# An attention and feed-forward layer in fp32: start of the first batch reordered (wq ahead of x, scaling folded into the halves of wq, bv times wo ahead of V, K's first copies issued by ScalarE)

## The chip, the cores and the metric

The kernel runs on one core of one Trainium2 chip. A core has five engines that run side by side: TensorE (PE in the profile, with PEld for its weight loads), VectorE (DVE), ScalarE (ACT), GpSimd (POOL) and SyncE (SP), which here only issues transfers. 16 DMA engines move data. The metric is device time in microseconds (us), lower is better. The kernel before takes 2871.87 us, the median of 3 runs (2871.01 to 2873.98).

## The reference

For each of 16 sequences of 512 rows and width 512:

```
q = layer_norm(x, ln1_g, ln1_b)
qh = (q @ wq + bq), kh = (ctx @ wk + bk), vh = (ctx @ wv + bv)   # 16 heads of 32
scores = qh @ kh^T / sqrt(32), causal mask, softmax
x1 = x + (probs @ vh) @ wo + bo
h = layer_norm(x1, ln2_g, ln2_b)
out = x1 + gelu(h @ w1 + b1) @ w2 + b2                            # inner width 2048
```

Everything is fp32.

## The kernel before

**Two stages.** stage_a does attention for all 16 batches and ends near 1480 us; stage_b does the feed-forward part. Only the start of stage_a is changed, the part that is done once, before and in the first batch.

**Precision.** Dense products are split: each fp32 operand is held as a high half in fp32r (made by a cast, _hi) and the remainder (_lo). A product is three matmuls: hi·hi, lo·hi, hi·lo. ScalarE makes the high halves (weight_high, x_high, qk_high), VectorE the low ones (weight_low, x_low, qk_low), GpSimd both for the context (context, lines 791 to 798).

**Folding of the layer norm's vectors.** ln1_g and the factor -1/sqrt(32) go into wq: before, VectorE writes wq_scaled (four instructions of 128x512 at line 615, in the space of v_sb), from which ScalarE casts wq_hi and VectorE makes wq_lo. ln1_b goes into a bias: TensorE multiplies the raw wq by ln1_b with 32 matmuls of one column (line 495, bias_mm), VectorE adds bq and scales (lines 630, 632). bv and bo are folded into one row: job B multiplies bv, spread over 128 columns (bvx), by the raw wo (line 383), and VectorE adds it to bo_row (line 673). The raw weights lie in buffers that are used for other things later: wq and wo share pT, wk has the rest of pT, wv has sm.

**Prologue.** The list PRO gives TensorE's order: X0 to X3 (transposes of the normalised rows, line 378), Q0, K0 (12 matmuls of 512 columns each, line 427), V0a (24 of 256 columns, line 422). Each job writes one of three banks bank_d in turn, and waits until the bank's last reader is done. ScalarE and VectorE have their own hand-written order of the same work. The queue of SP issues vec, x (four tiles), wq, two context tiles, wk, wv, bo, two more context tiles (each when its buffer is free), wo, then the copies for Q0 and K0.

**Stacks.** The scores take the three products at once: 96 rows stack hi, lo and hi of 32 features. So each Q0 or K0 (st_hi, st_lo) is copied into stack by three transfers of 256 KB (stack_parts, line 270): two from st_hi, once qk_high is done, and one from st_lo, once qk_low is done. The first score waits for all six.

**Batches.** A batch has 4 groups of 12 steps. At each step TensorE does the score of a tile, then its share of a dense job from BESIDE (in group 0 of the first batch: B, Q1, K1, V1a), then the transpose of the probabilities three tiles back. VectorE masks and takes the minimum (line 590), ScalarE takes the exponential (line 727). The copies for the next group's Q and K are issued as soon as they are made, and the next group's first score waits for them.

Of the kernel before, what the change touches and what calls it, by code (L numbers as in the profile page):

```python
# [20 lines left out]
F32 = mybir.dt.float32  # L21
# [31 lines left out]
def stage_a(nc, x, ctxT, wq, wk, wv, wo, vecs, bo, x1):  # L53
# [16 lines left out]


    COUNT = {"X": 4, "Q": 12, "K": 12, "V": 24, "R": 4, "O": 12, "B": 4}
    PRO = ["X0", "X1", "X2", "X3", "Q0", "K0", "V0a"]


    BESIDE = [
# [13 lines left out]
    def beside(groups, first, last):  # L90

        steps = [[] for _ in range(TG * len(groups))]
        for g, jobs in enumerate(groups):
            for job, at in jobs:
                if job == "R" and first and g == 0 or job == "B" and not first or job[0] == "O" and first:
                    continue
                if last and (job[0] == "X" or job in ("Q0", "K0", "V0a")):
                    continue
                done = 0
                for k, n in at.items():  # L100
                    steps[TG * g + k].append((job, done, done + n))
                    done += n
                assert done == COUNT[job[0]]
        return steps
# [3 lines left out]
    with ExitStack() as ctx:  # L108
# [11 lines left out]
        w_lo = [sb(f"{n}_lo", [P, KT, D], F32R) for n in ("wq", "wk", "wv", "wo")]  # L120
        vec = sb("vec", [P, 5, 4])
        bqs = sb("bqs", [P, NG])
        bo_row = sb("bo_row", [P, D])
        xt = sb("xt", [P, QT, D])
        xnT_hi = sb("xnT_hi", [P, KT, S], F32R)
# [25 lines left out]
        raw = [pT_flat[:, 0:KT * D], pT_flat[:, KT * D:2 * KT * D], sm[:].rearrange("p t n -> p (t n)"),  # L151
               pT_flat[:, 0:KT * D]]
        assert SLOTS_S * 512 == KT * D
        wq_scaled = v_sb[:].rearrange("p t n -> p (t n)")
        bvx = rT[:].rearrange("p (t m) -> p t m", t=KT)

        bank_s = [pb(f"bank_s{i}") for i in range(BANKS_S)]
# [100 lines left out]
        def _(sp):  # L258
# [23 lines left out]
            def load_x(m, t):  # L282
                sp.dma_start(xt[:, t, :], one(x_v, m)[:, t, :]).then_inc(x_in[t], 16)

            for t in range(QT):
                load_x(0, t)

            def load_weight(i):
                sp.dma_start(raw[i].rearrange("p (t n) -> p t n", t=KT),
                             (wq, wk, wv, wo)[i].rearrange("(t p) n -> p t n", p=P)).then_inc(raw_in[i], 16)  # L290

            load_weight(0)
            load_c(0, 0)
            load_c(0, 1)
            load_weight(1)
# [3 lines left out]
            load_c(0, 2)  # L299
            sp.wait_ge(c_done, 2)  # L300
            load_c(0, 3)
            sp.wait_ge(scaled, KT)
            sp.wait_ge(bias_mm, 1)
            load_weight(3)
            for w, job in enumerate(("Q0", "K0")):
                stack_parts(pro, w, job, 0, 0, 0)

            def stacks(it, g):

# [52 lines left out]
        def _(pe):  # L362
# [121 lines left out]

            pe.sem_inc(transposed, SLOTS_S)
            pe.sem_inc(pv_done, 2)
            pe.wait_ge(consts, 1)
            for job in PRO:
                if job == "Q0":

                    pe.wait_ge(vec_in, 16)
                    pe.wait_ge(raw_in[0], 16)
                    for g in range(NG):
                        for kt in range(KT):
                            mm = pe.matmul(bank_s[0][:, g:g + 1], raw[0][:, D * kt + P * g:D * kt + P * g + P],
                                           vec[:, 1, kt:kt + 1], start=(kt == 0), stop=(kt == KT - 1))
                    mm.then_inc(bias_mm, 1)
                    pe.wait_ge(w_lo_done, 1)
                if job == "K0":
                    pe.wait_ge(w_lo_done, 2)  # L500
                if job == "V0a":
                    pe.wait_ge(w_lo_done, 3)
                dense_step(pro, job, 0, 0, COUNT[job[0]])

            def body(it):
# [35 lines left out]
        def _(dve):  # L541
# [65 lines left out]
                dve.sem_inc(d_free[i], 1)  # L607
            dve.wait_ge(vec_in, 16)
            V.tensor_copy(bvx, vec[:, 4, :].unsqueeze(2).to_broadcast([P, KT, P])).then_inc(bvx_ok, 1)
            for t in range(QT):  # L610
                layer_norm_stats(0, t)
            dve.wait_ge(raw_in[0], 16)
            for kt in range(KT):

                V.tensor_scalar(wq_scaled[:, D * kt:D * kt + D], raw[0][:, D * kt:D * kt + D],
                                vec[:, 0, kt:kt + 1], -SCALE, ALU.mult, ALU.mult).then_inc(scaled, 1)
            for t in range(QT):
                normalise(0, t)

            def weight_low(i, done):  # L620
                dve.wait_ge(w_hi_done, i + 1)
                V.tensor_tensor(w_lo[i][:].rearrange("p t n -> p (t n)"), raw[i] if i else wq_scaled,
                                w_hi[i][:].rearrange("p t n -> p (t n)").bitcast(F32),
                                ALU.subtract).then_inc(done, 1)

            weight_low(0, w_lo_done)
            for t in range(QT):
                x_low(pro, f"X{t}", 0, 0)
            dve.wait_ge(bias_mm, 1)
# [1 line left out]
            dve.wait_ge(bias_ok, 1)  # L631
            V.tensor_scalar(bqs[:], bqs[:], -SCALE, None, ALU.mult).then_inc(scaled, 1)
            weight_low(1, w_lo_done)
            dve.wait_ge(scaled, KT + 1)
            qk_low(pro, "Q0", 0, 0)
            weight_low(2, w_lo_done)
            qk_low(pro, "K0", 0, 0)
            weight_low(3, wo_lo_done)
            dve.wait_ge(consts, 2)

            def body(it):
                for n in range(len(it.steps) + it.tail):
                    g, k = divmod(n, TG)
                    if (n > LAG and not it.tail or n <= LAG and not it.first) and not act_moves(n - LAG - 1):
                        move_tile(dve, V.tensor_copy, it, n - LAG - 1)
                    if not it.tail:
                        mask_and_max(it, n)
                    for job, jg in it.ended(n):
                        if job[0] == "X":
                            x_low(it, job, jg, it.b + 1)  # L650
                    beside_previous = g < NG and not (it.first and g == 0) and n < len(it.steps)
                    if k == 1 and beside_previous:

                        dve.wait_ge(probs, it.b * TB + TG * g)
                        V.reciprocal(recips[:, (g - 1) % 2, :], sums[:, (g - 1) % 2, :]).then_inc(recip_ok, 1)
                    if k == O_PROD_AT and beside_previous:
                        o_product(it, g - 1)
                    if not it.last and not it.tail:
                        for t in range(QT):
                            if (g, k) == STATS_AT[t]:  # L660
                                layer_norm_stats(it.b + 1, t)
                        for t in range(QT):
                            if (g, k) == NORMALISE_AT[t]:
                                normalise(it.b + 1, t)
                    for job, jg in it.ended(n - 1):

                        if job[0] in "QK":
                            qk_low(it, job, jg, it.b * NG + (jg + 1))
                    for job, jg in it.ended(n):
                        if job == "B":  # L670
                            dve.wait_ge(dense, it.done(job, jg))
                            dve.wait_ge(bo_in, 16)
                            V.tensor_tensor(bo_row[:], bank_d[it.bank(job, jg)][:], bo_row[:],
                                            ALU.add).then_inc(d_free[it.bank(job, jg)], 1)
                        if job[0] == "O":
                            t, bank = int(job[1]), it.bank(job, jg)
                            dve.wait_ge(dense, it.done(job, jg))

                            dve.wait_ge(res_ok, it.b * QT + (t + 1 - QT))
                            V.tensor_tensor(xt[:, t, :], bank_d[bank][:], xt[:, t, :],  # L680
                                            ALU.add).then_inc(d_free[bank], 1)
# [5 lines left out]
        def _(act):  # L687
# [54 lines left out]

            def weight_high(i):
                act.wait_ge(raw_in[i], 16)
                A.copy(w_hi[i][:].rearrange("p t n -> p (t n)"), raw[i] if i else wq_scaled).then_inc(w_hi_done, 1)

            act.wait_ge(scaled, KT)
            weight_high(0)
            for t in range(QT):
                x_high(pro, f"X{t}", 0)  # L750
            weight_high(1)
            act.wait_ge(scaled, KT + 1)
            qk_high(pro, "Q0", 0, 0)
            weight_high(2)
            qk_high(pro, "K0", 0, 0)
            weight_high(3)
            v_copy(pro, "V0a", 0)

# [29 lines left out]
        def _(pool):  # L788
# [23 lines left out]
            def o_low(it, g):  # L812
# [12 lines left out]

            G_.affine_select(out=mask[:, 384:512], in_=mask[:, 384:512], compare_op=ALU.is_ge, fill=MASKED, base=0,
                             pattern=[[-1, P]], channel_multiplier=1).then_inc(consts, 1)
            for fb in range(2):
                context(0, fb)
            inverse_root(0)  # L830
            for fb in (2, 3):
                context(0, fb)

            def body(it):
# [18 lines left out]
                expand(it, 2)  # L853
                o_low(it, 2)
                if it.first:
                    pool.wait_ge(d_free[it.bank("B", 0)], it.bank_read("B", 0))
                pool.wait_ge(res_in, it.b * 16 + 16)
                for t in range(QT):
                    G_.tensor_tensor(out=xt[:, t, :], in0=xt[:, t, :], in1=bo_row[:],
# [870 lines left out]
```

## Time and profile before

| | |
|---|---|
| median of 3 runs | 2871.87 us |
| the profiled execution | 2871.73 us |
| its span, first to last instruction | 2870.0 us |
| outside the span | 1.73 us |
| TensorE busy | 2766.4 us (96%) |
| VectorE, ScalarE, GpSimd busy | 70%, 58%, 12% |
| first matmul | 17.38 us |
| first score | 50.05 us |
| mean granted TensorE clock | 0.988 of 2.4 GHz |

A busy TensorE at 96% means that nearly all of the span is matmuls, one behind another; what can be taken out is found where TensorE is idle or works without need. That is read from the timeline (each instruction's start and duration), the list of who waited for whom, and the busy time of each engine in stretches. Matmul durations in the timeline overlap: of a row of equal matmuls, the distance from start to start is what one costs.

### The profile page before, as it was taken

To read this page: it belongs to the slowest core of one execution; us is meant where nothing else is said; L and a number is where in the kernel's file an instruction comes from. 1 tells how busy PE (TensorE), PEld (TensorE's weight loads), DVE (VectorE), ACT (ScalarE), POOL (GpSimd) and SP (SyncE) were. 2 spreads that over 40 slices of the span, in tenths; PEclk is the share of its full clock that TensorE was granted. 3 is DMA by queue.
4 is the path that set the end of the run, shared out by engine and by line. 5 is a ranking of instruction groups with operands and counts; after the bars stand their busy time and mean duration, and the time that the engine had idled before them with its cause. 6 is when DMAs were issued, how large, how long until landed. Compare 5 with 4: busy or idle time off the path is not lost. (4 is left out here: it accounts for less than half of the span.)

```text
span 2870.0 us, 65737 instructions
## 1 busy us (share of the span) xinstructions
PE 2766.4 (96%) x22056; PEld 2513.9 (88%) x22056; DVE 2016.5 (70%) x4852; ACT 1678.4 (58%) x4046; POOL 356.1 (12%) x364
## 2 busy tenths in 40 slices
PE   6999999999999999999957999999999999999999
PEld 4788888888888888888847999999999999999999
DVE  4777777776777777777648778778778755666566
ACT  3666666666766666666635655655665544444444
POOL 1211222112222222222110000000000000000000
PEclk9999999999999999999988999999999999999999
DMA  6667767776676667766632543443455334433342
GB/s 141 113 124 113 117 115 126 121 111 121 114 126 121 105 123 117 124 124 111 97 119 96 191 171 129 175 188 131 156 190 206 132 116 154 159 135 142 126 161 96
DMA packets 152506, 383.03 MB, mean 133 GB/s; under 512 B 12928, under 2 KB 17024, under 8 KB 144256
## 3 DMA queue, kind: packets, MB, share of 16 engines
q1 hardware_dynamic: 152448, 382.28, 54.5%
q8 instruction: 34, 0.56, 0.1%
q14 instruction: 24, 0.20, 0.0%
HBM read 172.51 MB, written 109.05 MB: 98 GB/s over the span
## 5 line engine op out<-in xcount | busy, mean ns | idle before, releaser
L727 ACT ACTIVATE sm<-sm,mins 128x128 f32<-128x128 f32 (+3 forms) x1024 | 572.2, 559 | 463.2 <-DVE mins L590 458.0
L590 DVE CUSTOM_DVE_ANT_0 sm<-bank_s,mask 128x128 f32<-128x128 f32 (+3 forms) x1024 | 475.5, 484 | 120.6 <-PE bank_s L442 118.8
L537 DVE COPY pT<-bank_t 128x384 f32<-128x384 f32 (+1 forms) x544 | 307.7, 566 | 240.1 <-PE bank_t L454 240.0
L454 PE MATMUL bank_t<-ident,sm 128*128 128x128 f32 x2560 | 412.7, 275 | 6.9 <-ACT pT L537 3.4
L454 PEld LDWEIGHTS bank_t<-ident,sm 128*128 128x128 f32 x2560 | 306.6, 140 | 87.9 <-issue 30.6
L442 PE MATMUL bank_s<-stack 96*128 96x128 f32 (+3 forms) x1024 | 352.8, 385 | 13.7 <-DMA stack<-st_lo 11.6
L1115 PE MATMUL bank_x<-b_hi,w_hi 128*128 128x256 f32 x1024 | 294.8, 288 | 18.0 <-ACT g L1538 9.6
L1115 PE MATMUL bank_x<-w_hi,a_hi 128*128 128x256 f32 x1024 | 291.2, 284 | 3.5 <-DVE a_lo L1235 3.5
L1117 PE MATMUL bank_x<-b_hi,w_lo 128*128 128x256 f32 x1024 | 291.7, 285 | 0.0
L1116 PE MATMUL bank_x<-b_lo,w_hi 128*128 128x256 f32 x1024 | 291.6, 285 | 0.0
L1116 PE MATMUL bank_x<-w_lo,a_hi 128*128 128x256 f32 x1024 | 290.8, 284 | 0.0
L1117 PE MATMUL bank_x<-w_hi,a_lo 128*128 128x256 f32 x1024 | 290.7, 284 | 0.0
L1549 ACT ACTIVATE g<-g,vecb 128x256 f32<-128x256 f32 x384 | 174.7, 503 | 111.3 <-DVE g L1316 109.3
L1563 ACT CAST a_hi<-g 128x512 fp32r<-128x512 f32 x256 | 158.7, 621 | 116.1 <-PE bank_x L1117 93.7
L1115 PEld LDWEIGHTS bank_x<-b_hi,w_hi 128*128 128x128 f32 x1024 | 198.1, 193 | 20.1 <-DVE w_lo L1235 11.4
L1115 PEld LDWEIGHTS bank_x<-w_hi,a_hi 128*128 128x128 f32 x1024 | 197.8, 193 | 4.0 <-DVE xr L1360 3.6
L1116 PEld LDWEIGHTS bank_x<-b_lo,w_hi 128*128 128x128 f32 x1024 | 198.5, 194 | 0.0
L1117 PEld LDWEIGHTS bank_x<-b_hi,w_lo 128*128 128x128 f32 x1024 | 198.4, 194 | 0.0
L1116 PEld LDWEIGHTS bank_x<-w_lo,a_hi 128*128 128x128 f32 x1024 | 197.8, 193 | 0.0
L1117 PEld LDWEIGHTS bank_x<-w_hi,a_lo 128*128 128x128 f32 x1024 | 197.7, 193 | 0.0
L727 ACT ACTIVATION_READ_ACCUMULATOR sm<-sm,mins 128x1 f32 x1024 | 192.1, 188 | 0.0
L442 PEld LDWEIGHTS bank_s<-stack 96*128 96x128 f32 x1024 | 175.0, 191 | 18.7 <-DMA stack<-st_lo 11.6
(178 smaller groups left out, 7423.8 us busy)
## 6 DMA issues: line engine op xcount, KB each, us to landing
stack<-st_hi SPq DMA_DIRECT2D x256, 256.0 KB, 6.1
stack<-st_lo SPq DMA_DIRECT2D x128, 256.0 KB, 8.1
xr<-x_scratch SPq DMA_DIRECT2D x32, 1024.0 KB, 5.9
b_scratch<-b_hi SPq DMA_DIRECT2D x16, 1792.0 KB, 9.9
b_scratch<-b_lo SPq DMA_DIRECT2D x16, 1792.0 KB, 13.7
b_hi<-b_scratch SPq DMA_DIRECT2D x16, 1792.0 KB, 7.4
b_lo<-b_scratch SPq DMA_DIRECT2D x16, 1792.0 KB, 11.2
xt<-in_x SPq DMA_DIRECT2D x64, 256.0 KB, 2.7
```

The source lines that it names most:

```text
L442: mm = pe.matmul(bank_s[n % BANKS_S][:, off:off + w], stack[0:96, g % 2, 0, r, P * qt:P * qt + P], stack[0:96, g % 2, 1, r, 0:w], start=Tr ...
L454: mm = pe.transpose(bank_t[n % 2][:, P * c:P * c + P], sm[:, n % SLOTS_S, P * c:P * c + P], ident[:])
L537: copy(out, src).then_inc(moved[n % 2], 1)
L590: op = V.tensor_tensor_reduce(sm[:, n % SLOTS_S, off:off + w], bank_s[n % BANKS_S][:, off:off + w], mask[:, 512 - w:512], 1.0, 0.0, ALU.ad ...
L727: op = A.activation(row, row, ACT.Exp, bias=mins[:, g % 2, c:c + 1], scale=-1.0, accum_out=sums[:, g % 2, c:c + 1])
L1115: pe.matmul(o, lh, rh, start=opens, stop=False, skip_group_check=True)
L1116: pe.matmul(o, lh, rl, start=False, stop=False, skip_group_check=True)
L1117: return pe.matmul(o, ll, rh, start=False, stop=True, skip_group_check=True)
L1549: op = A.activation(to, bank_x[d][:, C * m:C * m + C] if name == "C21" else to, ACT.Gelu, bias=vec[:, f:f + 1], scale=1.0)
L1563: A.copy(a_part(a_hi, k, h), a_source(k, h)).then_inc(a_hi_ok, 1)
```

## The change

Five edits, all in what is done once:

- SP issues wq ahead of the four tiles of x. TensorE's 32 matmuls for the bias (line 495) stand ahead of everything, in front of its wait for the constants.
- wq_scaled is gone. VectorE writes a vector wq_scale of 4 columns, ScalarE makes wq_hi in four activations of 128x512 with that scale, VectorE makes wq_lo in four scalar_tensor_tensor of 128x512, ahead of the layer norm's statistics.
- Job B moves from group 0 of the first batch into the prologue, between K0 and V0a; its addition to bo_row moves along.
- K0's copies are issued by ScalarE (stack_keys), not by SP. wv_hi is made ahead of Q0's high half.
- GpSimd takes the inverse root ahead of the context tiles; the load of wo waits for the halves of wq.

```
-    PRO = ["X0", "X1", "X2", "X3", "Q0", "K0", "V0a"]
+    PRO = ["X0", "X1", "X2", "X3", "Q0", "K0", "B", "V0a"]
...
             load_weight(0)
+            for t in range(QT):
+                load_x(0, t)
             load_c(0, 0)
...
-            sp.wait_ge(scaled, KT)
+            sp.wait_ge(w_lo_done, KT)
             sp.wait_ge(bias_mm, 1)
             load_weight(3)
-            for w, job in enumerate(("Q0", "K0")):
-                stack_parts(pro, w, job, 0, 0, 0)
+            stack_parts(pro, 0, "Q0", 0, 0, 0)
...
+            V.tensor_scalar(wq_scale[:], vec[:, 0, :], -SCALE, None, ALU.mult).then_inc(scaled, 1)
+            for kt in range(KT):
+                dve.wait_ge(w_hi_done, kt + 1)
+                V.scalar_tensor_tensor(w_lo[0][:, kt, :], raw[0][:, D * kt:D * kt + D], wq_scale[:, kt:kt + 1],
+                                       w_hi[0][:, kt, :].bitcast(F32), ALU.mult, ALU.subtract).then_inc(w_lo_done, 1)
             for t in range(QT):
                 layer_norm_stats(0, t)
...
+            def stack_keys():
+
+                def copy(part, src):
+                    act.dma_start(stack[32 * part:32 * part + 32, 0, 1, :, :].bitcast(F32),
+                                  src[:, 1, :].bitcast(F32)).then_inc(stacked, 16)
+
+                act.wait_ge(qk_hi, 2)
+                copy(0, st_hi)
+                copy(2, st_hi)
+                act.wait_ge(d_free[pro.bank("K0", 0)], pro.bank_read("K0", 0))
+                copy(1, st_lo)
+
+            act.wait_ge(scaled, 1)
+            act.wait_ge(raw_in[0], 16)
+            for kt in range(KT):
+                A.activation(w_hi[0][:, kt, :], raw[0][:, D * kt:D * kt + D], ACT.Identity, bias=0.0,
+                             scale=wq_scale[:, kt:kt + 1]).then_inc(w_hi_done, 1)
             for t in range(QT):
                 x_high(pro, f"X{t}", 0)
             weight_high(1)
-            act.wait_ge(scaled, KT + 1)
+            weight_high(2)
+            act.wait_ge(scaled, 2)
             qk_high(pro, "Q0", 0, 0)
-            weight_high(2)
             qk_high(pro, "K0", 0, 0)
+            stack_keys()
             weight_high(3)
             v_copy(pro, "V0a", 0)
...
-            for fb in range(2):
-                context(0, fb)
             inverse_root(0)
-            for fb in (2, 3):
+            for fb in range(KT):
                 context(0, fb)
```

## Rows read from the trace of the kernel before

**Rows 1.** Windows: stretch, length, busy us of PE, PEld, DVE, ACT, POOL, clock, DMA share, GB/s.
```profile
0.00:20.00 20.00, 2.62 (x12) 2.42 (x12) 10.03 (x19) 4.35 (x4) 7.74 (x15) 1.00 0.80 276
...
160.00:180.00 20.00, 20.00 (x139) 15.91 (x141) 13.72 (x43) 11.41 (x33) 0.61 (x1) 1.00 0.72 121
```

**Rows 2.** Waits of TensorE, 0 to 120 us: total, times, longest.
```profile
PE bank_d L378 <- DVE xt L560: 17.4, 1, 17.4
PE bank_s L442 <- DMA stack<-st_lo: 10.8, 3, 7.5
```

**Rows 3.** Timeline (start, duration, what, idle before) up to the inverse root.
```profile
7.70 0.69 DVE L547 BATCH_NORM_STATS2 stats<-xt 128x6 f32<-128x512 f32 x1 [0.84 <-DMA xt<-in_x]
...
8.76 0.17 DVE L555 TENSOR_SCALAR ve<-mv 128x4 f32<-128x4 f32 x1
10.78 3.06 DVE L615 TENSOR_SCALAR v_sb<-pT,vec 128x512 f32<-128x512 f32 x4 [1.85 <-DMA pT<-in_wq]
10.83 1.28 ACT L745 ACT_TABLE_LOAD   x1 [10.83 <-DMA pT<-in_wq]
...
15.62 1.02 POOL L803 TENSOR_TENSOR rstd<-ve,nhalf 128x4 f32<-128x4 f32 x1
```

**Rows 4.** The same timeline, the transposes of x and the bias.
```profile
17.38 2.79 PE L378 MATMUL bank_d<-ident,xt 128*128 128x128 f32 x12 [17.38 <-DVE xt L560]
18.50 0.59 ACT L693 CAST xnT_hi<-bank_d 128x512 fp32r<-128x512 f32 x1 [2.73 <-PE bank_d L378]
18.51 2.29 DVE L622 TENSOR_TENSOR wq_lo<-v_sb,wq_hi 128x2048 fp32r<-128x2048 f32 x1
18.63 2.64 POOL L795 CAST cT_hi<-c_raw 128x512 fp32r<-128x512 f32 x1 [1.99 <-DMA c_raw<-in_ctxT]
...
20.71 1.88 DVE L568 TENSOR_TENSOR xnT_lo<-bank_d,xnT_hi 128x512 fp32r<-128x512 f32 x3
...
22.36 6.83 PE L495 MATMUL bank_s<-vec,pT 128*128 128x1 f32 x32
...
23.23 0.69 DVE L568 TENSOR_TENSOR xnT_lo<-bank_d,xnT_hi 128x512 fp32r<-128x512 f32 x1 [0.63 <-ACT xnT_hi L693]
23.25 1.27 POOL L797 TENSOR_TENSOR cT_lo<-c_raw,cT_hi 128x512 fp32r<-128x512 f32 x1
```

**Rows 5.** The same timeline, Q0's first matmul to job B.
```profile
29.05 0.77 PE L427 MATMUL bank_d<-xnT_hi,wq_hi 128*128 128x512 f32 x1
...
34.62 0.69 ACT L703 ACTIVATE st_hi<-bank_d,bqs 128x512 fp32r<-128x512 f32 x1 [9.62 <-PE bank_d L427]
...
35.33 1.33 SPq L270 DMA_DIRECT2D stack<-st_hi  x2
...
40.11 0.55 SPq L270 DMA_DIRECT2D stack<-st_lo  x1
...
40.70 1.09 SPq L264 DMA_DIRECT2D c_raw<-in_ctxT  x2
...
50.05 0.80 PE L442 MATMUL bank_s<-stack 96*128 96x128 f32 x2 [7.46 <-DMA stack<-st_lo]
...
50.64 5.92 PE L383 MATMUL bank_d<-pT,rT 128*128 128x512 f32 x8
```

**Rows 6.** Windows: the wait for the first stack, and a later stretch at half clock.
```profile
37.50:48.00 10.50, 3.11 (x25) 2.91 (x24) 4.84 (x3) 3.06 (x3) 0.00 (x0) 0.86 1.07 132
...
76.00:79.00 3.00, 3.00 (x12) 2.51 (x11) 0.81 (x5) 1.61 (x6) 0.00 (x0) 0.50 0.01 3
```

**Rows 7.** Timeline: two matmuls of Q1, its copies, the second group's first score.
```profile
56.63 0.39 PE L427 MATMUL bank_d<-xnT_lo,wq_hi 128*128 128x512 f32 x1
56.86 0.40 PE L427 MATMUL bank_d<-xnT_hi,wq_lo 128*128 128x512 f32 x1
...
60.67 1.26 SPq L270 DMA_DIRECT2D stack<-st_hi  x2
...
74.36 0.50 PE L442 MATMUL bank_s<-stack 96*128 96x128 f32 x2 [2.39 <-DMA stack<-st_lo]
```

More of the change, by code:

```diff
@@ L94, in beside @@
             for job, at in jobs:
-                if job == "R" and first and g == 0 or job == "B" and not first or job[0] == "O" and first:
+                if job == "R" and first and g == 0 or job[0] == "O" and first:
                     continue
@@ L122, in stage_a @@
         bqs = sb("bqs", [P, NG])
+        wq_scale = sb("wq_scale", [P, KT])
         bo_row = sb("bo_row", [P, D])
@@ L153, in stage_a @@
         assert SLOTS_S * 512 == KT * D
-        wq_scaled = v_sb[:].rearrange("p t n -> p (t n)")
         bvx = rT[:].rearrange("p (t m) -> p t m", t=KT)
@@ L283, in load_x @@
                 sp.dma_start(xt[:, t, :], one(x_v, m)[:, t, :]).then_inc(x_in[t], 16)
-            for t in range(QT):
-                load_x(0, t)
             def load_weight(i):
@@ L486, in _ @@
             pe.sem_inc(pv_done, 2)
+            pe.wait_ge(vec_in, 16)
+            pe.wait_ge(raw_in[0], 16)
+            for g in range(NG):
+                for kt in range(KT):
+                    mm = pe.matmul(bank_s[0][:, g:g + 1], raw[0][:, D * kt + P * g:D * kt + P * g + P],
+                                   vec[:, 1, kt:kt + 1], start=(kt == 0), stop=(kt == KT - 1))
+            mm.then_inc(bias_mm, 1)
             pe.wait_ge(consts, 1)
@@ L489, in _ @@
                 if job == "Q0":
[L491 to L498, printed above, removed]
+                    pe.wait_ge(w_lo_done, KT)
                 if job == "K0":
-                    pe.wait_ge(w_lo_done, 2)
+                    pe.wait_ge(w_lo_done, KT + 1)
                 if job == "V0a":
-                    pe.wait_ge(w_lo_done, 3)
+                    pe.wait_ge(w_lo_done, KT + 2)
                 dense_step(pro, job, 0, 0, COUNT[job[0]])
@@ L609, in _ @@
             V.tensor_copy(bvx, vec[:, 4, :].unsqueeze(2).to_broadcast([P, KT, P])).then_inc(bvx_ok, 1)
+            V.tensor_scalar(wq_scale[:], vec[:, 0, :], -SCALE, None, ALU.mult).then_inc(scaled, 1)
[3 more added lines that the diff above has]
+                                       w_hi[0][:, kt, :].bitcast(F32), ALU.mult, ALU.subtract).then_inc(w_lo_done, 1)
             for t in range(QT):
                 layer_norm_stats(0, t)
[L612 to L616, printed above, removed]
             for t in range(QT):
@@ L620, in weight_low @@
             def weight_low(i, done):
-                dve.wait_ge(w_hi_done, i + 1)
-                V.tensor_tensor(w_lo[i][:].rearrange("p t n -> p (t n)"), raw[i] if i else wq_scaled,
+                dve.wait_ge(w_hi_done, KT + i)
+                V.tensor_tensor(w_lo[i][:].rearrange("p t n -> p (t n)"), raw[i],
                                 w_hi[i][:].rearrange("p t n -> p (t n)").bitcast(F32),
                                 ALU.subtract).then_inc(done, 1)
-            weight_low(0, w_lo_done)
             for t in range(QT):
@@ L633, in _ @@
             weight_low(1, w_lo_done)
-            dve.wait_ge(scaled, KT + 1)
+            dve.wait_ge(scaled, 2)
             qk_low(pro, "Q0", 0, 0)
@@ L637, in _ @@
             qk_low(pro, "K0", 0, 0)
+            dve.wait_ge(dense, pro.done("B", 0))
+            dve.wait_ge(bo_in, 16)
+            V.tensor_tensor(bo_row[:], bank_d[pro.bank("B", 0)][:], bo_row[:],
+                            ALU.add).then_inc(d_free[pro.bank("B", 0)], 1)
             weight_low(3, wo_lo_done)
@@ L669, in body @@
                     for job, jg in it.ended(n):
[L670 to L674, printed above, removed]
                         if job[0] == "O":
@@ L744, in weight_high @@
                 act.wait_ge(raw_in[i], 16)
-                A.copy(w_hi[i][:].rearrange("p t n -> p (t n)"), raw[i] if i else wq_scaled).then_inc(w_hi_done, 1)
-            act.wait_ge(scaled, KT)
-            weight_high(0)
+                A.copy(w_hi[i][:].rearrange("p t n -> p (t n)"), raw[i]).then_inc(w_hi_done, 1)
+            def stack_keys():
[9 more added lines that the diff above has]
+            act.wait_ge(raw_in[0], 16)
+            for kt in range(KT):
+                A.activation(w_hi[0][:, kt, :], raw[0][:, D * kt:D * kt + D], ACT.Identity, bias=0.0,
+                             scale=wq_scale[:, kt:kt + 1]).then_inc(w_hi_done, 1)
             for t in range(QT):
@@ L855, in body @@
                 if it.first:
-                    pool.wait_ge(d_free[it.bank("B", 0)], it.bank_read("B", 0))
+                    pool.wait_ge(d_free[pro.bank("B", 0)], pro.bank_read("B", 0))
                 pool.wait_ge(res_in, it.b * 16 + 16)
```

2 rows, old and new, of the table BESIDE are left out of this document.

## The prediction

> **What bounds the kernel now.** I read the windows first. From 160 us on TensorE is busy through all of a 20 us stretch, in the first 20 us it has 2.62 us of work [rows 1]: the steady part is bound by TensorE, the start by what comes before it. So a microsecond taken from the start should be kept to the end, and nothing else in this change touches the steady part. Then the list of TensorE's waits: 17.4 us for the first normalised rows, and 10.8 us for the low parts of stacks, 7.5 of it once, before the first score [rows 2]. Then the timeline, to follow what each of these two waits for.
>
> The first wait: x has landed at 7.70, the variance is ready at 8.93, but the inverse root runs on GpSimd only from 15.62 to 16.64 [rows 3], behind two context tiles. The transposes start at 17.38. The low part of X0 starts only at 20.71, since VectorE makes wq_lo until then (18.51 to 20.80), and X3's transposes wait for it. x is finished at 23.92, but TensorE is in the 32 small bias matmuls from 22.36 [rows 4], and Q0 starts at 29.05 [rows 5].
>
> The second wait: Q0's copies are issued at 35.33, K0's last at 40.11, the first score starts at 50.05 [rows 5]. In between the DMA engines are full (share 1.07) and move 132 GB/s [rows 6]: six copies of 262 KB are 1.57 MB, 11.9 us at that rate, and with the time to the first byte and to the last signal they make 14.7 us from Q0's issue to the score. So the score hangs on when Q0's copies start, not on when K0's last one does. The second group repeats this: from Q1's copies at 60.67 to its first score at 74.36 are 13.7 us, with TensorE idle for the last 2.39 [rows 7].
>
> **Part 1: wq first, its halves and the inverse root.** In the kernel before x takes until 7.70 and wq 3.1 us more, until 10.78 [rows 3]. Turned round, wq lands between 5.5 (7.70 less part of the slow start) and 7.70, and x at about 10.8. I take 7.0 for wq. ScalarE's table load, 1.28 [rows 3], and four activations of about 0.6 to 0.7 (0.69 is the row of the same kind from PSUM [rows 5]) follow; VectorE ends the fourth low part 0.75 after the last: 7.0 + 1.3 + 2.7 + 0.8 = 11.8 (10.3 to 12.6). The statistics now stand behind that: four at 0.69, then 0.54 to the end of the variance [rows 3]: 15.1. GpSimd's root no longer stands behind context tiles: 16.2. Before it was 16.64. So a gain of 0.4; the bounds are x's landing (10.8 with three statistics done, a gain of 1.9) and a loss of 0.4. Transposes start at 17.0.
>
> VectorE has no wq_lo to do behind them, so X0's low part follows its high part, ready at 19.09, instead of 20.71: the stretch from first transpose to last low part, 6.54, shrinks by 1.6 to 4.9 [rows 4]. That ends at 21.9 and Q0 starts at 22.0, where before it started at 29.05: 7.0 earlier. The terms are 0.4 + 1.6 + 5.1 (the bias matmuls that stuck out behind x, 23.92 to 29.05). The bias matmuls now take 7.0 to 14, when TensorE has nothing else; if wq landed late, they would start to cost only beyond 10.
>
> GpSimd's context tiles are what pays for the root: they start at 16.2 instead of 11.5, and the next two loads are issued that much later. Before, the last ended at 24.52, with 2 us of waiting and a cast that took 2.64 us while VectorE ran wq_lo [rows 4]. So it ends between 24.5 and 29.4, I take 27. K0 needs it for its tenth matmul, about 29.8. No cost, but with only 3 us of cover.
> On that cast: 2.64 us beside a VectorE instruction of 2.29 [rows 4]. The Trainium skill (SBUF — State Buffer, "SBUF: two separate sides") says VectorE with two SBUF inputs and GpSimd lock each other out for a whole instruction. The trace agrees; by that rule wk_lo could stop one tile again, which is within the bound.
>
> **Part 2: Q0 to the first score.** Q0's twelve matmuls at half clock took 5.57 to its high part, 34.62 from 29.05, and 0.71 more to the copies [rows 5]. If it goes the same, the copies are issued at 22.0 + 6.3 = 28.3 to 28.4, against 35.33: 6.9 earlier. The clock could rise earlier in it; at the most it saves some 1.3 us. wv_hi, now ahead of Q0's high part, ends on ScalarE at about 25, under Q0.
>
> K0 ends at about 30.7, its high part is ready at 31.5, its low part at 32.3 behind wv_lo. By then the three copies of Q0 (6 us of DMA time from about 30.4) still run, so K0's copies come in time to keep the engines full, and again the sum of the transfers sets the end. ScalarE issuing them costs it about 0.6 us each, as SP's rows show [rows 5], under B and V0a: nothing.
> What is new: SP no longer waits for K0, so it issues the two context tiles for the next batch (at 40.70 before, behind all copies [rows 5]) right behind Q0's copies, ahead of K0's. They are 0.52 MB. If other lanes carry them they cost nothing; at the 276 GB/s of the first 20 us [rows 1] they cost 1.9. I take 0.6, nearer to none since loads move at more than twice the rate of the copies. First score: 28.4 + 14.7 + 0.6 = 43.7, a gain of 6.35. The 14.7 itself may be 13.7, as for the second group [rows 7].
> No row has a transfer issued by ScalarE. The Trainium skill (DMA: Bandwidth & Descriptors, "Issuing engines are not separate DMA queues") says that both run on the same 16 engines and only issue time is saved. By it this part brings nothing, which is also what my sum has; were it wrong, K0's 6 us would overlap Q0's (rival C).
>
> **Part 3: B.** It ran from 50.64 at half clock and held TensorE for 5.6 us between the first score and Q1. It now runs behind K0, at full clock (some 3.5 us), from 30.7 to 34.3; V0a follows to 37.1, both under the wait for the stack. wo is issued at about 21 and has landed. But its going doesn't give all of it, since the half clock that B sat in is now spent on Q1: from the first score to Q1's copies were 10.62 us (50.05 to 60.67 [rows 5, 7]). Now: 0.4 for the score, twelve matmuls at half clock (twice the 0.23 from start to start at full clock [rows 7], less a hair: 5.1), 0.4 for the second score, 0.9 to the copies: 6.8. A gain of 3.8. The second group hangs on these copies by 13.7 us, so this gain counts on. TensorE's own work in group 0 ends at about 62.5, before the stack at 64.3.
>
> **Sum.** 6.35 + 3.8 = 10.1 us. From the third group on nothing is left that the change touches. The profiled execution has 2871.73 (span 2870.0 and 1.73 outside), 0.14 under the median; 2871.87 - 10.1 = 2861.8.
> What can move without the change: in 76 to 79 us TensorE stood at half clock after the 2.39 us wait [rows 6, 7]; half of such a stretch of 3 us is 1.5. It may be there or not. Likewise the wait before the first score is now 37.1 to 43.7, 6.6 us against 7.46; if the clock does not fall in it, Q1 runs at full clock and 2.7 more are gained.
>
> **Rivals.**
> A, only the front part arrives. wq shares the engines with x and lands no earlier than 10.78. Then the halves end at 15.6, the root at 20.0, transposes start at 20.8, and Q0 at 25.8: 3.2 gained there, 7.0 in all with B's 3.8, or 2864.9. The same size comes if the context tiles hold K0 until 31 or later. For it: x and wq overlapped partly, as the bandwidth in the start is uneven; against it: x, issued first, landed 3.1 us ahead.
> B, the front is gained but B's leaving is not, because the second group's start hangs on something other than Q1's copies, K1's last copy or TensorE's own work: 6.35 to 7, 2865.2. Against it: 2.39 us of idle with all DMA engines full.
> C, more than the sum: x's landing and not VectorE sets the root (1.5), the clock stays up at the first score (2.7), K0's copies overlap Q0's (up to 6, of which TensorE's own work in group 0 lets 2 through at the second group). One or two of these: 13 to 16, 2857.
> D, slower. If a transfer issued by ScalarE held that engine until it landed (9.9 us for K0's last copy, 40.11 to 50.05 [rows 5]), three would hold it from 31.5 to 61; the first exponential, then V0a's copy and wo_hi all wait. Exponentials start at 64 against 51.7, and the second group, which needs Q1's high part from ScalarE, starts about 6 later than before: 2878. It turns slower from about 8 us held per copy. Against it: SP issues the next copy 0.6 us after the last, 1.33 for two [rows 5].
>
> **How the numbers follow.** The forecast (gain 8.5 to 12) 0.50, A 0.14, B 0.10, C 0.19, D 0.02; 0.05 for other losses that leave a gain under 5.7. Range: from C's 2857 to A and B with 1.9 for the context loads, 2867. 0.2% is 5.7 us, about what can be told from no change: faster is below 2866.1. A and B lie at 7 and pass under 5.7 in a fifth of their cases, 0.05. Faster 0.88, same 0.09, slower 0.03.
>
> **What would show it.** Bias matmuls from about 7; wq_lo done at 12; root at 15 to 16; transposes at 17; Q0 at 22; no wait of K0 for contexts; Q0's copies at 28.4; ACT's queue issuing three copies at 31 to 33; B at 0.43 us from start to start; first score at 43.7 and the second group's at 64.3 (before: 50.05, 74.36). It is wrong if the root comes after 18, if the DMA share between the issue and the score is well under 1, or if the shift at 160 us isn't the one at 64.

## The result: slower, by what lies behind the start

The changed kernel takes 2880.44 us (median of 7 runs, 2877.6 to 2883.83) against 2871.6 (2867.58 to 2873.98): a ratio of 1.0033, 95% interval 1.0021 to 1.0045. The forecast was 2861.8. The profiled execution took 2877.6 us, the quickest of the seven; its span is 2875.9, so again 1.7 lie outside. So it is 8.8 us slower, 0.33%, where 10.1 us of gain were forecast.

The start went nearly as forecast. The timeline of the changed kernel (start, duration, what, idle before), from the halves of wq to the first score:

```profile
7.12 6.96 PE L489 MATMUL bank_s<-vec,pT 128*128 128x1 f32 x32 [7.12 <-DMA pT<-in_wq]
...
9.10 2.74 DVE L610 SCALAR_TENSOR_TENSOR wq_lo<-pT,wq_scale,wq_hi 128x512 fp32r<-128x512 f32 x4 [5.78 <-ACT wq_hi L757]
...
14.84 1.02 POOL L814 TENSOR_TENSOR rstd<-ve,nhalf 128x4 f32<-128x4 f32 x1 [12.64 <-DVE ve L552]
15.81 0.61 POOL L806 CAST cT_hi<-c_raw 128x512 fp32r<-128x512 f32 x1
15.89 4.37 DVE L557 TENSOR_SCALAR xt<-xt,mv,rstd 128x512 f32<-128x512 f32 x4 [1.14 <-POOL rstd L814]
16.50 1.33 POOL L808 TENSOR_TENSOR cT_lo<-c_raw,cT_hi 128x512 fp32r<-128x512 f32 x1
...
23.53 0.77 PE L425 MATMUL bank_d<-xnT_hi,wq_hi 128*128 128x512 f32 x1 [1.49 <-DVE xnT_lo L565]
...
29.15 1.33 SPq L270 DMA_DIRECT2D stack<-st_hi  x2
...
31.19 1.09 SPq L264 DMA_DIRECT2D c_raw<-in_ctxT  x2
31.90 1.33 ACTq L745 DMA_DIRECT2D stack<-st_hi  x2
...
33.27 0.64 ACTq L745 DMA_DIRECT2D stack<-st_lo  x1
33.95 1.90 ACT L740 CAST wo_hi<-pT 128x2048 fp32r<-128x2048 f32 x1 [2.08 <-issue]
...
45.50 0.80 PE L440 MATMUL bank_s<-stack 96*128 96x128 f32 x2 [8.06 <-DMA stack<-st_lo]
```

Q0 starts at 23.53 against 29.05, its copies go out at 29.15 against 35.33, and the first score is at 45.50 against 50.05 [rows 5]. The second group's first score is at 67.02 against 74.36 [rows 7], 7.3 us ahead. Then the lead turns into a lag: at 207 us, in the second batch, it is still 5.6 us (the rows at 212.21 and 206.59 in the next section but one), and at stage_b it is gone. The first transfer of stage_b, in the timelines of SP's queue, before and after:

```profile
1488.13 0.35 SPq L1035 DMA_DIRECT2D vecb<-in_vecs_b  x1
```

```profile
1494.50 0.35 SPq L1044 DMA_DIRECT2D vecb<-in_vecs_b  x1
```

So some 14 us are lost between 67 and 1494 us, in code whose instructions are the same. Behind the start the waits of TensorE from 100 to 1470 us (total, times, longest) show where. Before:

```profile
PE bank_d L427 <- DVE xnT_lo L568: 4.0, 15, 0.3
...
PE bank_s L442 <- DMA stack<-st_lo: 0.9, 1, 0.9
```

After:

```profile
PE bank_s L440 <- DMA stack<-st_lo: 12.7, 15, 1.1
PE bank_d L425 <- DVE xnT_lo L565: 3.9, 15, 0.3
```

Once in each of 15 batches TensorE now waits for a stack, and these waits are 11.8 of the 14 us. The list of DMA queues and issues from 100 to 1400 us shows the transfers (for the queue: packets, MB, share of the engines' time; for the copies: count, KB each, median us to landing). Before, then after:

```profile
q1 hardware_dynamic: 83376, 153.13, 70.0%
...
stack<-st_hi SPq DMA_DIRECT2D x236, 256.0 KB, 6.1
stack<-st_lo SPq DMA_DIRECT2D x118, 256.0 KB, 8.1
```

```profile
q1 hardware_dynamic: 82688, 151.86, 71.9%
...
stack<-st_hi SPq DMA_DIRECT2D x232, 256.0 KB, 6.6
stack<-st_lo SPq DMA_DIRECT2D x116, 256.0 KB, 8.7
```

Fewer bytes take more of the engines' time, 71.9% of it instead of 70.0%, and the copies land later. Since the same transfers are asked for, three causes were open: where the tensors lie in memory, the second queue, or a worse rhythm of the loop.

**What had moved.** Each tensor of a stage is placed behind the one declared before it, its size rounded up to 32 bytes per partition. The change declares wq_scale (16 bytes) between bqs and bo_row. In the kernel before bo_row, xt, c_raw, st_hi, st_lo and stack all lay at multiples of 256 bytes (stack at 137472); in the changed kernel they lie 32 bytes past one (stack at 137504). stage_b's tensors are placed anew and didn't move.

### The profile page after: what moved, and what is told of

The parts are those of the page before. It is cut to its first block and busy times, and to the rows that moved or that the text cites. A ratio compares the mean times of both kernels' runs of the same rounds, so it can differ in the third digit from the quotient of the medians.

```text
span 2875.9 us, 65740 instructions
## 1 busy us (share of the span) xinstructions
PE 2766.7 (96%) x22056; PEld 2511.5 (87%) x22056; DVE 2016.4 (70%) x4852; ACT 1681.5 (58%) x4049; POOL 353.7 (12%) x364
## 5 line engine op out<-in xcount | busy, mean ns | idle before, releaser
L440 PE MATMUL bank_s<-stack 96*128 96x128 f32 (+3 forms) x1024 | 353.6, 386 | 25.4 <-DMA stack<-st_lo 25.4
## 6 DMA issues: line engine op xcount, KB each, us to landing
b_scratch<-b_lo SPq DMA_DIRECT2D x16, 1792.0 KB, 13.7
b_lo<-b_scratch SPq DMA_DIRECT2D x16, 1792.0 KB, 11.2
```

What stands on the lines that cost most here:

```text
L440: mm = pe.matmul(bank_s[n % BANKS_S][:, off:off + w], stack[0:96, g % 2, 0, r, P * qt:P * qt + P], stack[0:96, g % 2, 1, r, 0:w], start=Tr ...
```

## The experiments

In all of them the ratio is to the kernel before on the same chip, with its 95% interval.

**e1, wq_scale declared last.**

```
-        wq_scale = sb("wq_scale", [P, KT])       # between bqs and bo_row
...
         nhalf = sb("nhalf", [P, QT])
+        wq_scale = sb("wq_scale", [P, KT])
```

> The changed kernel with one line moved: the tensor wq_scale is declared last instead of between bqs and bo_row, so that every tensor behind it lies where it lay in the kernel before (xt, c_raw, st_hi, stack at multiples of 256 bytes; the change had put them 32 bytes past such a multiple). Same instructions, same order. Theory P (place in memory: each copy between badly placed tensors takes the DMA engines longer, in every group of every batch): stack copies land in 6.1 and 8.1 us again instead of 6.6 and 8.7, TensorE's wait for stacks falls from 25.4 us to about 8, and the gain of the start is kept: 2861 to 2865 us. Theory R (a second queue, ScalarE's, once used, slows all transfers of the first): nothing changes, 2880. Theory S (the shifted start puts the loop in a worse rhythm of transfers and matmuls): 2880 too.

Measured: 2863.16 us, 0.9973 (0.9963 to 0.9983). Every engine's list of instructions is that of the changed kernel, and it is 17.3 us faster. The waits and copies, 100 us on:

```profile
PE bank_d L425 <- DVE xnT_lo L565: 3.9, 15, 0.3
PE bank_s L440 <- DMA stack<-st_lo: 3.0, 5, 1.0
```

```profile
q1 hardware_dynamic: 83068, 152.56, 69.8%
...
stack<-st_hi SPq DMA_DIRECT2D x234, 256.0 KB, 6.1
stack<-st_lo SPq DMA_DIRECT2D x117, 256.0 KB, 8.2
```

That is theory P, and it already speaks against S: the shifted start with well-placed tensors keeps its lead. One number of the expectation missed: over the whole program the wait for stacks fell from 25.4 to 13.7 us and not to about 8, since 10.7 of it lie in the first 120 us, where the first stacks are waited for in any case.

**e2 and e3, the kernel before with an unused tensor.**

```
         bqs = sb("bqs", [P, NG])
+        pad = sb("pad", [P, 8])      # e2: 32 bytes; e3: [P, 64], 256 bytes
```

> The kernel before with an unused tensor of 32 bytes per partition declared between bqs and bo_row, nothing else. Theory P: slower by what the change lost behind its start, some 15 to 17 us: about 2887 us; stack copies land in 6.6 and 8.7 us. Theories R and S: the instructions are those of before, so 2871.6.

> The kernel before with an unused tensor of 256 bytes at the same place: all tensors move, but by a multiple of 256 bytes. Theory P in the form that the remainder by 256 bytes decides: 2871.6, copies at 6.1 and 8.1 us. If any shift does harm, for instance because the tensors come to lie otherwise to each other or to a boundary further out: about 2887. Theories R and S: 2871.6.

Measured: 2888.94 us, 1.0065 (1.0051 to 1.0079) with 32 bytes, and 2870.42, 1.0002 (0.9993 to 1.0011) with 256. A tensor that no instruction touches costs 18 us, and eight times as much of it costs nothing. Where it goes, e2's waits from 100 to 1470 us:

```profile
PE bank_s L443 <- DMA stack<-st_lo: 11.9, 15, 1.2
```

and its queue and copies from 100 to 1400 us:

```profile
q1 hardware_dynamic: 82634, 151.80, 72.0%
...
stack<-st_hi SPq DMA_DIRECT2D x234, 256.0 KB, 6.1
stack<-st_lo SPq DMA_DIRECT2D x117, 256.0 KB, 7.5
```

Here the expectation missed: the copies land in 6.1 and 7.5 us, not in 6.6 and 8.7, though the time and the waits are those of bad placement. So the median landing doesn't tell the placements apart (in e8, with stack at a multiple of 256, it is 6.1 and 7.7). What does is the engines' share for the same bytes: 71.9 to 72.0% for 151.6 to 151.9 MB in the four kernels with stack 32 bytes off (changed, e2, e4, e5), 69.6 to 70.0% for 152.6 to 153.1 MB in all with stack at a multiple of 256.

**e4, K0's copies by SyncE, tensors 32 bytes off.**

```
-            stack_parts(pro, 0, "Q0", 0, 0, 0)
+            for w, job in enumerate(("Q0", "K0")):
+                stack_parts(pro, w, job, 0, 0, 0)
...
-            stack_keys()
```

> The changed kernel with K0's three copies issued by SyncE behind Q0's, as before; the tensors stay 32 bytes off. Theory R: all of the later loss goes, about 2862 us. Theory P: the later loss stays, 2880 us, within 2 us of the changed kernel. The first score moves little in either, since the sum of the transfers sets it: 44 to 46 us.

Measured: 2880.37 us, 1.0037 (1.0023 to 1.005), as the changed kernel. Without any use of the second queue the loss is all there: theory R falls.

**e5 and e6, one side of the copies.**

```
+        pad = sb("pad", [P, 8])      # e6: here
         st_hi = sb("st_hi", [P, 2, S], F32R)
         st_lo = sb("st_lo", [P, 2, S], F32R)
+        pad = sb("pad", [P, 8])      # e5: here
         stack = sb("stack", [P, 2, 2, 4, S], F32R)
```

(with 224 bytes behind the shifted tensors, so that all others keep their remainder)

> The kernel before with only stack, the destination of the copies, 32 bytes past a multiple of 256 (an unused 32 bytes ahead of it and 224 behind it, so all else keeps its place or its remainder). If writes to a badly placed row are what costs: all of the loss of the shift of everything, about 2888 us. If reads cost: 2871. If both halves cost alike: about 2880.

> The kernel before with only st_hi and st_lo, the sources of the copies, 32 bytes past a multiple of 256; stack back at a multiple. If reads from a badly placed row are what costs: about 2888 us. If writes cost: 2871. Both alike: about 2880. If neither this nor the destination alone costs, it is the loads and stores of x and context: then both give 2871.

Measured: destination off 2887.71 us, 1.0056 (1.0042 to 1.0069); sources off 2871.48, 0.9999 (0.999 to 1.0008). The loss comes with the place of stack alone; that of the sources costs nothing. x and the context lay well in both; as e2, with everything off, lost 18.1 us and e5 16.4, with intervals that overlap, nothing is left that would have to be theirs. TensorE too reads stack, but its matmuls from it take 385 ns in the mean in before, e2 and e5 alike (100 to 1400 us), so it is the copies' writes that are slower. In 64 to 72 us, while the second group's copies and one load of x keep the DMA engines full (length, busy times, clock, DMA share, GB/s), before and e5:

```profile
64.00:72.00 8.00, 7.74 (x68) 6.37 (x66) 7.21 (x21) 5.96 (x16) 0.00 (x0) 1.00 1.08 136
```

```profile
64.00:72.00 8.00, 6.11 (x55) 4.81 (x53) 6.74 (x20) 6.24 (x16) 0.00 (x0) 1.00 1.06 126
```

126 against 136 GB/s: 7% less, at a share that is 2% lower.

**e7 and e12, other remainders.**

```
         bqs = sb("bqs", [P, NG])
+        pad = sb("pad", [P, 32])     # e7: 128 bytes; e12: [P, 16], 64 bytes
```

> The kernel before with everything behind bqs at a remainder of 128 bytes instead of 0. If a remainder is harmful because a row of 2048 bytes then touches nine blocks of 256 bytes instead of eight, 128 costs as 32 does: 2888 us. If only remainders by 64 or 128 bytes matter: 2871. If the bytes ahead of the row in its first block cost too, more than 2888.

> The kernel before with everything behind bqs at a remainder of 64 bytes by 256. With 32 it lost 16 us and with 128 3 us or nothing. If 64 bytes is the unit within which a written row must start: 2871 to 2875. If it is 128 bytes: about 2888, as with 32. If the loss falls off by degrees: near 2880.

Measured: 128 bytes 2874.63 us, 1.0008 (0.9999 to 1.0017); 64 bytes 2878.35, 1.0029 (1.0017 to 1.0041). So the loss falls off by degrees, and no single unit explains it. The same window as above, for e7 and then e12, lies between the two, at 130 and 129 GB/s:

```profile
64.00:72.00 8.00, 7.12 (x63) 5.86 (x61) 7.19 (x20) 5.75 (x16) 0.00 (x0) 1.00 1.08 130
```

```profile
64.00:72.00 8.00, 6.76 (x60) 5.47 (x58) 7.20 (x21) 5.66 (x15) 0.00 (x0) 1.00 1.07 129
```

Two stretches of the timelines leave the jitter of the start out. One set of six copies is measured from the issue of Q1's first copy to the second group's first score, which in every kernel waits for the last of them. The loop alone runs from the third group's first score to stage_b's first transfer:

| kernel | stack past a multiple of 256 | one set of copies | third group's score | stage_b's first transfer | loop |
|---|---|---|---|---|---|
| before | 0 | 13.69 | 94.69 | 1488.13 | 1393.4 |
| e3, 256 bytes | 0 | 13.62 | 90.95 | 1484.10 | 1393.2 |
| e6, sources 32 off | 0 | 13.63 | 90.82 | 1483.81 | 1393.0 |
| e1, wq_scale last | 0 | 13.80 | 85.35 | 1480.51 | 1395.2 |
| e8 | 0 | 13.67 | 85.24 | 1477.86 | 1392.6 |
| e9 | 0 | 13.69 | 88.75 | 1481.20 | 1392.5 |
| e10 | 0 | 13.67 | 83.78 | 1478.54 | 1394.8 |
| e11 | 0 | 13.81 | 89.64 | 1483.11 | 1393.5 |
| e7 | 128 | 14.03 | 95.00 | 1490.32 | 1395.3 |
| e12 | 64 | 14.27 | 95.06 | 1496.20 | 1401.1 |
| e2 | 32 | 14.43 | 95.59 | 1503.02 | 1407.4 |
| e5, stack alone | 32 | 14.44 | 94.84 | 1505.10 | 1410.3 |
| changed | 32 | 14.60 | 88.08 | 1494.50 | 1406.4 |
| e4 | 32 | 14.65 | 85.78 | 1493.73 | 1408.0 |

The set of copies takes 13.6 to 13.8 us at a multiple of 256, 14.0 at 128, 14.3 at 64 and 14.4 to 14.7 at 32: the grading is there already in a single set, 0.3, 0.6 and 0.7 to 1.0 us over before. The loop multiplies it unevenly, with 2, 8 and 13 to 17 us. At a multiple of 256 the eight loops lie between 1392.5 and 1395.2, so the 1395.3 at 128 is hardly told from them, as its time isn't told from no loss by its interval; in its waits the place does show (5.6 us for stacks, against 0.8 in e3).

**e8, stage_b's tensors at multiples of 256 too.** In e1:

```
+        pad = sb("padb", [P, 32])
         w1_hi = sb("w1_hi", [P, 7, 2, D], F32R)
```

> The changed kernel with wq_scale last, and 128 unused bytes ahead of stage_b's tensors, which lay at a remainder of 128 bytes in all kernels so far, so that they lie at multiples of 256. If stage_b's transfers gain as stack copies did (some 8%), b_hi lands in about 7.0 instead of 7.4 us and b_lo in 10.5 instead of 11.2; time falls only where TensorE waits for transfers there, which it hardly does: 2858 to 2863 us. No effect of place there: 2863.

Measured: 2863.61 us, 0.9974 (0.9963 to 0.9984), no gain over e1; b_hi lands in 7.4 us and b_lo in 11.1, against 7.5 and 11.2 in e1. These tensors were 128 bytes off, the mildest remainder, and their transfers are no copies to 32 partitions.

**e9, e10, e11: the parts of the gain, each undone in e1.** e9 puts B back in group 0 (its addition to bo_row with it), e10 lets SyncE issue K0's copies (e4's edit), e11 loads x ahead of wq.

```
-    PRO = ["X0", "X1", "X2", "X3", "Q0", "K0", "B", "V0a"]     # e9
+    PRO = ["X0", "X1", "X2", "X3", "Q0", "K0", "V0a"]
...
-        [("Q1", {0: 6, 1: 6}), ("K1", {2: 6, 3: 6}), ...
+        [("B", {0: 4}), ("Q1", {0: 6, 1: 6}), ("K1", {2: 6, 3: 6}), ...
...
```

```
-            load_weight(0)                                     # e11
             for t in range(QT):
                 load_x(0, t)
+            load_weight(0)
```

> The changed kernel with wq_scale last and job B back in group 0 of the first batch, where it was before. By the sum of the prediction B's move is worth 3.8 us, at the second group's first score: about 2867 us, that score at 68.6 instead of 64.8 us and the first score unmoved. If the second group hangs on something else than Q1's copies (rival B): 2863.

> The changed kernel with wq_scale last and K0's copies issued by SyncE. The prediction has this part at nothing gained and 0.6 us lost to the context tiles that now go ahead of the copies: 2862.5 us, first score at about 44.2 instead of 44.8. If a second queue lets copies overlap, it is slower than 2863.

> The changed kernel with wq_scale last and x loaded ahead of wq again, all else changed: the case of the prediction's rival A, wq landing at 10.8 us. Transposes then start at 20 to 21 us instead of 16.6, Q0 near 26 to 27 instead of 23.3: 3 to 4 us slower, 2866 to 2867. If the first score doesn't hang on Q0: 2863.

Measured: e9 2866.39 us, 0.9985 (0.9976 to 0.9994); e10 2862.55, 0.9968 (0.9957 to 0.998); e11 2866.45, 0.9988 (0.9979 to 0.9997). Against e1's 2863.16, B's move is worth 3.2 us, wq ahead of x 3.3, and ScalarE's issue -0.6, within the spread. e1 ran on another chip than these three, and the medians of the kernel before there are 2870.86 and 2871.42; so the two 3 us are good to 1 or 1.5 us. The traces agree with them in sign: the second group starts 3.3 us later in e9 and 4.5 later in e11 (69.32), where Q0 starts at 27.45, just past the expected 27. In e9 B stands where it stood:

```profile
44.60 0.80 PE L440 MATMUL bank_s<-stack 96*128 96x128 f32 x2 [9.13 <-DMA stack<-st_lo]
45.19 5.19 PE L381 MATMUL bank_d<-pT,rT 128*128 128x512 f32 x8
49.82 0.79 PE L425 MATMUL bank_d<-xnT_hi,wq_hi 128*128 128x512 f32 x1
```

and its second group starts at 68.17 us, in e1 at 64.85. e10's first score is at 43.31 us with Q0's copies out at 28.61, 14.7 later as in the kernel before; e1 needs 15.5 (29.30 to 44.79). e10 is the fastest kernel of this study, but not told from e1.

## Why the prediction was wrong

**The step that failed** is the first paragraph's claim that "nothing else in this change touches the steady part", and the sum's "from the third group on nothing is left that the change touches". The diff adds a tensor, and I costed the instructions around it and never its place. That moved stack by 32 bytes, and every copy to it in 16 batches with it: 17.3 us (e1 against the changed kernel). The prediction put this at nothing without a reason. Its own last sign of being wrong, that the shift at 160 us isn't the one at 64, is what came: 7.3 us ahead at 67 and 5.6 at 207. No rival held it, rival D least of all: an engine held by its transfers was not seen (33.95 is the start of wo_hi, 0.04 after the issue).

**The second failure is in reading.** "TensorE busy through all of a 20 us stretch" was taken as a bound by TensorE with room beside it. There was none at one place per batch. In the timeline of before, second batch, the group whose copies queue behind two context tiles and 1 MB of x:

```profile
212.21 1.21 SPq L270 DMA_DIRECT2D stack<-st_hi  x2
```

```profile
226.62 0.49 PE L442 MATMUL bank_s<-stack 96*128 96x128 f32 x2 [0.41 <-DVE mins L590]
```

14.4 us from copies to score. The last of the six, issued at 217.51, landed 9.0 us later, at 226.5; TensorE had come there at 226.21. In the changed kernel the same place:

```profile
206.59 1.21 SPq L270 DMA_DIRECT2D stack<-st_hi  x2
```

```profile
221.64 0.49 PE L440 MATMUL bank_s<-stack 96*128 96x128 f32 x2 [1.00 <-DMA stack<-st_lo]
```

15.05 us, and a wait of 1.00 for the stack. 0.8 us in each of 15 batches make the 12.7 of the list of waits. A wait of 0.9 us in all before was no sign of slack, only of copies that came just in time. The window over those copies, in the kernel before, has the DMA engines nearly full (share 0.97) beside a full TensorE:

```profile
212.00:226.00 14.00, 13.92 (x130) 11.53 (x128) 10.73 (x34) 9.67 (x28) 2.71 (x4) 1.00 0.97 137
```

**The sum for what the change meant to do** held in the main, in e1, where the tensors lie well; it gained 7.7 us of the 10.1:

- wq at 7.0, halves done at 11.8: 6.76 (start of the table load) and 11.55. Root at 16.2: 15.56, since the four statistics took 2.47 and not 2.76.
- Q0 at 22.0: 23.24, 1.2 late. Transposes came early, at 16.55 instead of 17.0, but the stretch from the first transpose to the last low part, which was to shrink by 1.6 to 4.9 us, took 6.54 as before: this term was nothing. The rows of e1:

```profile
16.55 1.09 PE L376 MATMUL bank_d<-ident,xt 128*128 128x128 f32 x4 [2.77 <-DVE xt L557]
...
22.40 0.69 DVE L565 TENSOR_TENSOR xnT_lo<-bank_d,xnT_hi 128x512 fp32r<-128x512 f32 x1 [0.63 <-ACT xnT_hi L688]
```

  GpSimd's first two context tiles now run beside the normalisation, and VectorE took 4.37 us for four instructions (row at 15.89 above; 4.38 in e1), where in the kernel before four took 1.92 with GpSimd idle. The prediction had the context tiles as a danger for K0 alone (they were done in time, K0 followed Q0 without a gap). The Trainium skill (SBUF — State Buffer, "SBUF: two separate sides") states that the ports which VectorE and GpSimd share are locked for a whole instruction, for VectorE in a mode with two ports as well as with two SBUF inputs. The trace agrees, 4.37 us against 1.92, though no row shows the mode; and I had applied it only to the instruction that it had hit before.
- Copies at 28.4 and first score at 43.7: 29.30 and 44.79; from one to the other 15.5 against 15.3. The 0.6 for the context tiles was 0.8 by e10. Rival C's overlap of two queues isn't there; the Trainium skill (DMA: Bandwidth & Descriptors, "Issuing engines are not separate DMA queues"), by which a second issuer saves issue time alone, agrees with e10 (2862.55 against 2863.16 us).
- B, 3.8: 3.3 at the second group's score and 3.2 in time (e9). The prediction's 5.6 us for B between the first score and Q1 is 5.36 in the trace (50.64 to 56.00); the sum doesn't use it. Rival A's loss against the forecast, 3.1: 3.3 (e11).
- Second group at 64.3: 64.85, after a first score that was 1.1 late, since from that score to Q1's copies were 6.3 us and not 6.8. It is a lead of 9.5 on before's trace. The median gained 7.7. Part of the difference is that the trace of before had a late start: e3 has the same instructions, and yet

```profile
21.98 4.93 PE L496 MATMUL bank_s<-vec,pT 128*128 128x1 f32 x32
```

the bias matmuls took 4.93 us instead of 6.83 [rows 4], Q0's copies went out at 32.49 instead of 35.33, and its second group started at 70.61; e6 had 70.51. So a gain at the start, read against one trace of the kernel before, can hold 3 to 4 us of luck.

Had the new tensor been declared last, the forecast of 2861.8 would have been 1.4 us off and in its range. Part of that closeness is luck, too: the kernel before had a median of 2870.86 beside e1, 1.0 under the one that the forecast starts from.

**What stays open.** Why a write to stack costs by degrees, 32 bytes more than 64 and 64 more than 128, isn't shown. The Trainium skill (DMA: Bandwidth & Descriptors, "How a descriptor splits into AXI transactions") says that a transfer is cut at multiples of 256 bytes and that a read from between them starts at the multiple below; an estimate worked out from this is that a row of 2048 bytes off such a multiple touches nine blocks instead of eight. That the remainder by 256 is what counts agrees with e3. But by it reads would suffer, and 128 as much as 32, and neither is so here: e6 lost nothing, e7 3 us or nothing. How much of each loss the loop adds is open as well: one set of copies is 0.3, 0.6 and 0.7 to 1.0 us slower at 128, 64 and 32 bytes, the loop loses 2, 8 and 13 to 17. Nor was stack tried at 64 or 128 by itself.

## What to carry to other kernels

A declaration is part of a change: a small tensor put between others moves all that follow. This kernel hangs on copies within SBUF once per batch, and there the remainder of their destination by 256 bytes was worth 17 us, twice what the new start was worth (7.7). Declare small tensors last, or round them up, and compare the addresses of before and after as one compares instructions. And before calling the steady part untouched, look in one batch for the transfer that arrives last and how long ahead of its reader.

## What the hardware showed that was not expected

- With the DMA engines full of copies from 128 to 32 partitions, in rows of 2048 bytes, they moved 136 GB/s with the destination at a multiple of 256 bytes and 130, 129 and 126 to 127 with it 128, 64 and 32 bytes past one (before, e7, e12, e5 and e2, 64 to 72 us). 32 bytes past in the source: no effect on the time (e6).
- VectorE's normalisation took 4.37 us with GpSimd's context tiles beside it and 1.92 without, as the timelines have it; no run took only the tiles away.
- TensorE's clock can rise at other moments in the same code. X3's transposes, ahead of the bias matmuls, in before and in e3:

```profile
21.45 1.12 PE L378 MATMUL bank_d<-ident,xt 128*128 128x128 f32 x4 [1.29 <-DVE xnT_lo L568]
```

```profile
21.49 0.66 PE L379 MATMUL bank_d<-ident,xt 128*128 128x128 f32 x4 [1.28 <-DVE xnT_lo L569]
```

  e3 then stood at half clock, 1.2 GHz, from 24 to 30 us, with Q0's matmuls 0.43 us from start to start, and they came to 0.23 at 31.06, still in Q0; in before that came at 35.02, in K0. The first scores are 3.4 us apart (46.65 and 50.05). For the same distance of 0.43 us the row of before says 1.00, so in this early stretch the level is to be read from the distance, not from the column of the clock. The rows (length, busy times, clock, DMA share, GB/s) of e3 and then of before:

```profile
24.00:30.00 6.00, 6.00 (x23) 5.32 (x23) 2.52 (x3) 0.56 (x1) 0.56 (x1) 0.50 0.27 86
```

```profile
30.00:34.00 4.00, 4.00 (x11) 3.08 (x10) 1.79 (x1) 0.00 (x0) 0.00 (x0) 1.00 0.79 262
```
